# GpSimd takes the second norm ahead of an expert's first low part; the first turns of GpSimd and VectorE in another order

## What is computed

```python
k = layernorm(x)                         # over the 512 features
v = ctx                                  # 16 x 128 x 512
# per feature, along the 128 steps of time, in a stable form:
#   y_t = (sum_{s<t} e^{w(t-1-s)+k_s} v_s + e^{u+k_t} v_t)
#       / (sum_{s<t} e^{w(t-1-s)+k_s}     + e^{u+k_t})
x1 = x + y
xn = layernorm(x1)
probs = softmax(xn @ gate_w.T)           # 8 experts, the best 2 are kept
moe = sum over the 2 of  p_e * (silu(xn @ G_e) * (xn @ U_e)) @ D_e      # 256 wide
shared = sigmoid(xn @ g) * (silu(xn @ Gs) * (xn @ Us)) @ Ds             # 1024 wide
out = x1 + moe + shared
```

## Time and profile before

| | |
|---|---|
| median of 3 runs | 552.39 us (552.17 to 553.98) |
| the profiled execution | 554.43 us, of which the span from the first to the last instruction is 552.6 us |
| TensorE matmul busy | 476.1 us, 86% of the span, 3293 instructions |
| TensorE weight load busy | 318.0 us, 58% |
| VectorE busy | 419.0 us, 76%, 932 instructions |
| ScalarE busy | 289.1 us, 52%, 579 instructions |
| GpSimd busy | 338.0 us, 61%, 431 instructions |
| mean clock granted to TensorE | 0.975 of full speed |

### The profile page before, as it was taken

One profiled execution on the slowest core, in us unless ns is written; L12 is line 12 of the kernel. 1 busy time (PEld: TensorE's weight loads), 2 busy tenths in 40 slices (PEclk: granted clock), 3 DMA queues, 4 the chain that ended last, 5 costly groups with the idle time before them and its releaser, 6 DMA issues.

```text
span 552.6 us, 11301 instructions
## 1 busy us (share of the span) xinstructions
PE 476.1 (86%) x3293; PEld 318.0 (58%) x3293; DVE 419.0 (76%) x932; ACT 289.1 (52%) x579; POOL 338.0 (61%) x431
## 2 busy tenths in 40 slices
PE   0036568999999999899999998999999999999991
PEld 0024345777767677677676776745545555555540
DVE  5879789898989899889899666766655666666661
ACT  4768475478587685785863755423332333333320
POOL 5676647875858858858586563505465655555442
PEclk9999697999999999999999999999999999999997
DMA  7982011131333314313232301414566866766644
GB/s 281 365 317 87 19 38 46 34 98 40 135 98 103 135 41 165 97 40 135 78 134 61 136 3 52 115 60 79 100 114 123 142 121 111 128 113 123 106 59 57
DMA packets 25933, 59.22 MB, mean 107 GB/s; under 512 B 6314, under 2 KB 6314, under 8 KB 24338
## 3 DMA queue, kind: packets, MB, share of 16 engines
q0 software_dynamic: 9824, 20.90, 21.3%
q1 hardware_dynamic: 16050, 37.59, 19.4%
HBM read 37.83 MB, written 20.65 MB: 106 GB/s over the span
## 4 chain that ended last, share of the span: by engine, by line
PE 26%; DMA 7%; DVE 7%; issue 6%; POOL 4%; SPq 3%; ACT 2%; POOLq 0%; ACTq 0%; DVEq 0%
PE GU L1028 11%; PE DN L1043 5%; DMA out<-wall,cb 5%; PE GU L1067 4%; SPq L389 3%; PE DN L1083 2%; PE XT L971 2%; DMA xb<-xn_rows,cb 1%; PE HS L971 1%; DVE wall L1269 1%; POOL wall L485 1%; DMA out<-xb 1%; DVE th L1382 1%; ACT junk L666 1%; DVE hx L1389 1%
## 5 line engine op out<-in xcount | busy, mean ns | idle before, releaser
L1067 PE MATMUL GU<-xt,wall 128*128 128x256 f16 x1536 | 191.4, 276 | 3.7 <-DVE HS L1384 2.3
L1067 PEld LDWEIGHTS GU<-xt,wall 128*128 128x128 f16 x1536 | 150.2, 99 | 35.9 <-DVE HS L1384 2.7
L641 POOL DMA_INDIRECT out<-wall,cb x39 | 62.0, 1590 | 77.6 <-DVE wall L1654 38.3
L1083 PE MATMUL DN<-wall,hx 128*128 128x512 f16 x384 | 95.7, 386 | 2.4 <-DVE hx L1389 2.1
L736 ACT ACTIVATE th<-GU,scl 128x256 f32<-128x256 f32 x103 | 48.6, 472 | 87.0 <-PE GU L1067 46.0
L1389 DVE TENSOR_TENSOR hx<-HS,hx 128x256 f16<-128x256 f32 x103 | 43.0, 418 | 62.9 <-ACT hx L745 62.9
L745 ACT ACTIVATE hx<-HS 128x256 f16<-128x256 f32 x103 | 39.1, 379 | 94.8 <-PE HS L971 61.0
L1028 PE MATMUL GU<-wall,kb 128*128 x240 | 61.4, 379 | 0.2 <-DVE kb L1585 0.2
L1083 PEld LDWEIGHTS DN<-wall,hx 128*128 128x128 f16 x384 | 37.4, 99 | 38.3 <-DVE hx L1389 4.1
L1028 PE MATMUL GU<-wall,xnb 128*128 x228 | 58.5, 379 | 0.4 <-DVE xnb L1585 0.4
L1382 DVE SCALAR_TENSOR_TENSOR th<-th,GU 128x256 f32<-128x256 f32 x103 | 41.7, 405 | 21.2 <-ACT th L736 21.2
(11 more groups left out here) (174 smaller groups left out, 795.2 us busy)
## 6 DMA issues: line engine op xcount, KB each, us to landing
wall<-wgu SPq DMA_DIRECT2D x12, 1024.0 KB, 5.6
wall<-wd SPq DMA_DIRECT2D x12, 512.0 KB, 7.3
out<-xb SPq DMA_DIRECT2D x20, 256.0 KB, 2.3
xb<-x SPq DMA_DIRECT2D x16, 256.0 KB, 2.9
cb<-ctx_t SPq DMA_DIRECT2D x16, 256.0 KB, 2.7
xn_rows<-xnb SPq DMA_DIRECT2D x16, 256.0 KB, 2.1
xb<-xn_rows,cb POOLq DMA_INDIRECT x39, 4.3
out<-wall,cb POOLq DMA_INDIRECT x39, 4.9
```

Source lines behind the costliest of these rows:

```text
L641: pool.indirect_dma_start(out, bass.IndirectOffsetOnAxis(ap=idsa[:, j:j + 1], axis=0), ye[j % RESULTS], None, compute_op=ALU.add).then_inc ...
L1067: ins = nc.tensor.matmul(GU[n % 2][:, g * 2 * P:(g + 1) * 2 * P], gate_up(sh_base(u // 2), wp, c)[:, f:f + P], xt_pair(n // PU * 2, xp, c) ...
L1083: ins = nc.tensor.matmul(DN[a][:], hx[n % 2][:, hp * IE + a * P:hp * IE + (a + 1) * P], down(sh_base(u // 2), wp, u % 2), start=u == 0 and ...
```

## The change

On GpSimd the waits for `nd` ahead of `quotient(0)` and of `shared_d_lo(1)` go away; `quotient(2)` stands ahead of `shared_d_lo(0)` and no longer behind it; in each turn `norm(i - 1, 1, ...)` stands ahead of `expert_lo(lo_e, 1)`. On VectorE `scan_e(2)` stands ahead of `shared_gu_lo(0)`, and `hidden(3, 1, SHARED)` ahead of the last two reciprocals of tile 3, `act_lo(2)` and the small steps. The same instructions run as before.

```diff
--- before.py
+++ after.py
@@ -543,7 +543,6 @@
                                     ALU.mult).then_inc(scale_step, 1)
             first_product(1)
             second_product(1)
-            pool.wait_ge(nd, 2)
             quotient(0)
             first_norm_steps(2)
             quotient(1)
@@ -555,11 +554,10 @@
             second_product(2)
             first_product(3)
             second_product(3)
+            quotient(2)
             shared_d_lo(0)
-            quotient(2)
             mean(4)
             first_norm_steps(4)
-            pool.wait_ge(nd, 4)
             shared_d_lo(1)
             norm(2, 1, agg2, norm2, xn_rdy)
             mean(5)
@@ -575,9 +573,9 @@
 
                 pool.wait_ge(nd, i + 1)
                 pool.wait_ge(masked, (i - 2) * 2)
+                norm(i - 1, 1, agg2, norm2, xn_rdy)
                 if lo_e is not None:
                     expert_lo(lo_e, 1)
-                norm(i - 1, 1, agg2, norm2, xn_rdy)
                 if i == LAG + 1:
                     shared_d_lo(2)
                 if lo_e is not None:
@@ -1439,8 +1437,8 @@
             first_stats(3)
             act_lo(0)
             dve.wait_ge(consts, CONSTS)
+            scan_e(2)
             shared_gu_lo(0)
-            scan_e(2)
             act_lo(1)
             scan_ev(2)
             add_now(2)
@@ -1465,10 +1463,10 @@
             reciprocals(3, 0, 2)
             hidden_lo(2, 0)
             keys(4)
+            hidden(3, 1, SHARED)
             reciprocals(3, 2, 2)
             act_lo(2)
             small_steps(1, 0)
-            hidden(3, 1, SHARED)
 
             def turn(i, j, sq_e, hi_e, ws_e, lo_e):
                 n = j * SU
```

## The result

The changed kernel took 556.96 us in the median of 5 runs (556.45 to 561.14), against 552.88 us for the kernel before on the same chip: ratio 1.0093, 95% interval 1.0052 to 1.0134. It is slower, and lies outside the range. Beside the kernel before on two other chips it gave 1.0150 and 1.0144.

What follows compares the result with a forecast made beforehand. TensorE is nearly full from 83 us, so time changes only in the four slices ahead or in small stalls. First turns 0.75 minus turn 15's 0.3 gives +0.45 us on the 552.39 us median: 552.8 us, range 550.0 to 555.8 us.

Steps and rivals of the forecast that it cites:

- The waits taken away: GpSimd's wait ahead of shared_d_lo(1) was called free: ScalarE's scaled weights, not add_now(3), ended its 3.33 us of idle time.
- The norm edit: Turns 7, 9, 11, 13: stalls of 0.42 and 0.40 us go, y_back's grows from 0.62 to 1.4 us; zero gain.
- The bound of +0.1 us a period: Upper bound for norm ahead of the first low part in turns 7 to 13; the lower was minus 0.6 us.
- quotient(0): Issued near 25.3 us instead of starting at 28.86 us, queued ahead of scan_ev(1), both over 2 us; bounds zero and 1.2 us.
- D: Delay of add_now(2) on VectorE in the first turns, 0.3 to 1.1 us, taken as 0.75 us and reaching unit 3.
- quotient(2): Ahead of shared_d_lo(0): y 2.9 us earlier minus D, mean(4) 0.35 us plus D later; gain becomes idle time before ranks(0).
- The clock's rival: TensorE's clock falls in new idle time ahead of keys_t(4) and ranks(0): 3.9 us on the chain, 556.7 us, chance 0.12.
- The other sign against the forecast: TensorE's ranks(0) starting before 69 us would show the forecast wrong; near 70.2 us would show it right.
- Turn 15: With the norm first, the first low part is in the way some 0.3 us earlier: -0.3 us, bounds -0.5 and 0.
- The sum: Over the whole kernel: 0.75 us from the first turns minus 0.3 us at turn 15, +0.45 us, giving 552.8 us.

Runs made afterwards that it cites:

- the repeat: The changed kernel run again, unaltered, beside the kernel before and the changed kernel with both waits put back: ratio 1.0150.
- the first turns alone: The changed kernel with norm and low part back in their old order, only the first turns changed: ratio 1.0044 to the kernel before.
- The kernel with the collision and without the late add: The changed kernel with two long-met waits (nd 2 and nd 4) put back behind all turns, ahead of the gathers: ratio 1.0082 to the kernel before.

## Why the prediction was wrong

- **The waits taken away (failed).** "The wait ahead of shared_d_lo(1) is free either way" holds for the wait itself, and the sum gave fewer instructions no price, with no bound for it. This is the step that failed. Two waits fewer on GpSimd cost 0.7% with nothing reordered (1.0070), by delays at turn 7's scatter and at the first add; with one or more of them put back as instructions the changed kernel is at 1.0008 to 1.0034, where it had 1.0093 to 1.0150. I took the trace of before as showing all of GpSimd's costs, though its later instructions would all lie elsewhere in the code.
- **The norm edit (right by itself, wrong in company).** The two short stalls went and came back in y_back's, 1.74 to 1.77 us instead of the 1.4 forecast, at the forecast spacing of 36.9 us. The bound of +0.1 us a period was wrong for one period: it asked whether the norm's input is ready, and not what VectorE issues beside the small step at the end of the chain. In the repeat that step made y_back(7) 0.8 us late against the changed kernel with both waits back (158.21 against 157.42 us), and y_back(9) as much. In the first profile y_back(9) was 2.61 us late, 1.24 us of it at y_back(7); the other 1.4 us came of the low clock behind it, which none of the four later profiles with the same stall had, so that part was chance.
- **quotient(0) (pattern right).** It was issued at 24.54 us at once behind second_product(1) and took 2.18 us, and both scans beside it took 2.2 us. add_now(2) came at 46.83 us, ahead of its 47.17; but the start of the run shifts by such amounts: y_back(3) lies at 84.86 us and 83.69 us in two executions of the kernel before, and at 83.83 and 85.74 us in two kernels that differ in three met waits. So the 0.75 us for D can't be read from it.
- **quotient(2) (right as to what passes on).** y at 57.67 us, mean(4) at 60.59 us, 0.25 us ahead of its old place where 0.35 us and D behind it were forecast, inside the shift of the start named above, and the gain handed on as idle time ahead of keys_t(4) (1.86 us) and ranks(0) (1.27 us).
- **The clock's rival (happened, and did not decide).** Behind ranks(0) six matmuls took 2.74 us at a grant of 0.50, where they took 1.46 us before. y_back(3) was 0.94 us late, and y_back(5) 0.04 us. The other sign against the forecast, ranks(0) ahead of 69 us, came too, at 68.73 us; but the kernel before has 68.32 us in its second execution, so it tells nothing. The rival's 556.7 us is near the result by chance.
- **Turn 15.** Its 0.3 us can't be told beside the rest; not tried.
- **The sum** of +0.45 us fits what the moved work costs: 1.0008 with both waits back. With an interval of 0.0026 to either side, 1.4 us, the measurement can't confirm it. The rest, 1.4% where both ran side by side (1.0150 against 1.0008), goes with the two instructions that are gone: the delays at the scatter and the add, and the collision that the first of them brings about.

What stays open: how much the late add costs in all. Two waits less gives 0.7%, the first turns alone 0.4%, while the add itself is 1.2 to 1.5 us late and 0.3 to 0.6 us longer. The kernel with the collision and without the late add has 1.0082, though its y_back(9) is only 0.8 us late; where the rest goes is not known. And TensorE's stall ahead of the gathered rows' first matmuls, near 360 us, costs the changed kernel 1.6 us in the first pair of profiles (1.78 against 0.22 us), but is 2.58 us in another profile of the kernel before, so it is not put down to the change.

## What to carry to other kernels

An edit that takes instructions out of an engine moves all that follows it in that engine's code, and can delay a critical instruction hundreds of microseconds later. Before an edit is blamed, run it with the number of instructions restored (a wait that is long met will do, if it is an instruction of its own), and compare where the packets of the instruction queues lie. And ask of each instruction put first in a row of work that is the bound whether its input is there: the low part ahead of the norm hid a wait of 0.75 us that the scatters had hidden before.

## What the runs showed of the hardware that was not expected

- Where GpSimd's instructions lie in its code can cost time: with two fewer, 0.30 us more ahead of a scatter and 1.2 to 1.5 us more ahead of an indirect DMA with an add, each with a packet of an instruction queue beside it.
- A wait put ahead of an instruction that waits for two semaphores added no instruction (11298), one ahead of an instruction with one did (11299).
- A tiny operation (2 to 16 values per partition) takes 0.15 to 0.25 us alone, and 1.1 us where the other of the two engines has issued a large one first. Which is first was decided by 0.13 us.
- The clock stayed at full behind the stalls of 1.75 us. Behind a stall of 2.93 to 2.95 us the grant was 0.50 in one execution and full in four others.
